# A graph layer on one core: rows copied before edges, scatters that wait for products, transposes moved behind a half's products

## The chip, the cores and the metric

The kernel runs on one core of one Trainium2 chip. A core has a matrix engine (TensorE, PE in the rows), a vector engine (VectorE, DVE), a scalar engine (ScalarE, ACT), GpSimd (POOL) and a queue engine (SyncE, SP). Each works through its own list of instructions in order; they meet through counters that an instruction raises at its end and another waits for. The metric is the device time of one execution in microseconds (us), lower is better.

## The reference

For 100,000 edges between 6,250 nodes, each with 128 features, a message is made from the source row, the destination row and the edge's own features, and the messages of a node are added up:

```python
row, col = (edge_index[0], edge_index[1])
msg_in = jnp.concatenate([x[row], x[col], edge_attr], axis=-1)
h = msg_in @ W + b
mu = jnp.mean(h, axis=-1, keepdims=True)
var = jnp.mean(jnp.square(h - mu), axis=-1, keepdims=True)
h = (h - mu) * jax.lax.rsqrt(var + LN_EPS) * gamma + beta
msg = jax.nn.relu(h)
out = jax.ops.segment_sum(msg, row, num_segments=x.shape[0])
# and around it: x = _layernorm(x + out)
```

The edges come sorted by `dst` (`col`), not by `src` (`row`), by which they are summed.

## The kernel before, in words

**Tables.** W is cut in three: x times its first third (`tabA`) and x times its second third (`tabB`) are made once, for 6,250 nodes. What is left for each edge is its own 128 features times the last third, plus two table rows.

**Groups and halves.** The edges are taken in 98 groups of 1,024 (`g` from 0 to 97), each as two halves of 512 (`h` 0 and 1); `t = 2 * g + h` counts halves. For a half:

- TensorE transposes the edges (`turn_edges`, L856, counter `e_turned`), ScalarE copies them from PSUM to SBUF (`copy_edges`, L1145, counter `eT_ready`), TensorE multiplies them by the weights and adds the `tabB` rows of a window by a 0/1 matrix (`edges_times_w`, L962 and L969, counter `h_done`). I call the result the half's products.
- ScalarE copies the products into `stage` (`stage_rows`, L1149, counter `st_ready`), and a number for each row (`number_rows`, L1139).
- Places for the rows in a DRAM array `rows`, sorted by blocks of source nodes, are worked out: VectorE makes one-hot matrices, TensorE ranks them (`ranks_from_base`, L844 and L846), VectorE makes positions (L1534, L1540, L1546).
- When a whole group is staged, GpSimd writes it with eight indirect DMAs of 128 rows each (`scatter`, L683). I call these eight a burst.

**Pairs.** Eleven groups (22 halves) later, while further edges are multiplied, the sorted rows are read back in pairs of units, `s = t - 22`. For a pair, TensorE turns the selectors (`turn_selectors`, L930), ScalarE copies them (`copy_selT`, L1175), TensorE picks `tabA` rows with them (`select_tile`, L940), VectorE adds these to the rows (L1564), ScalarE sums squares (L1183) and takes roots (L1189), VectorE makes messages (L1580), and TensorE sums them by node (`sum_tile`, L916). VectorE adds the sums to a table (L1556). After the last group comes a drain of the remaining pairs and the last layer norm.

**What sets the order.** Nothing is scheduled by a tool: each engine's `step` is written out by hand for all 98 groups, and the text of `step` is the order. Rings of four buffers hold edges, windows and staged rows; the edge loads run three groups ahead (`AHEAD`). The lines that wait, and that the change touches, are these:

```python
pool.wait_ge(st_ready, 2 * g + (1 if early else 2))     # scatter, GpSimd
pe.wait_ge(eT_ready, 2 * g + h + 1)                     # edges_times_w, TensorE
pe.wait_ge(st_ready, 2 * g + h - 1)
act.wait_ge(e_turned, 2 * g + h + 1)                    # copy_edges, ScalarE
act.wait_ge(h_done, 2 * g + h + 1)                      # stage_rows, ScalarE
```

The `Else` branches are for inputs whose destinations do not fit the windows; the input here takes the first branch.

## Time and profile before

| | |
|---|---|
| device time, median of 3 runs | 1757.65 us (1756.3 to 1757.97) |
| the profiled execution | 1758.61 us, its span 1756.8 us |
| busy share of the span | PE 68%, weight loads 60%, DVE 54%, POOL 44%, ACT 40% |
| granted TensorE clock, mean | 0.812 of full speed |
| chain that ended last | PE 39%, unknown queue 24%, issue 18%, ACT 10% |

No engine is busy all the time, so the time lies in how they wait for each other. The rows further down are read from the profile of this one execution. "Idle before" is how long an engine stood still ahead of an instruction, and the name behind the arrow is what ended it; "issue" means that nothing in the profile did, "remote" that the counter was raised by something the profile cannot name.

### The profile page before, as it was taken

Reading aid. Unit: us, or ns where it says so; the run is one execution under the profiler, and the core shown is the slowest. Engines: PE = TensorE matmul, PEld = TensorE weight load, DVE = VectorE, ACT = ScalarE, POOL = GpSimd, SP = SyncE. Lnnn points to the kernel's source line nnn. Section 1 sums busy time; section 2 is a strip of 40 time slices with the busy share of each in tenths; the row PEclk is TensorE's granted clock in tenths of the full one; section 3 lists DMA queues with packets and bytes.
Section 4 is the critical chain, followed back from the end, with each engine's and each line's share of the span. In section 5 each row is a group of like instructions: output and inputs, shape, how many; then the busy total and the mean of one; then the engine's idle time right before and its main releaser. Section 6 shows DMA issues by size and latency. Waiting matters only on the chain.

```text
span 1756.8 us, 36181 instructions
## 1 busy us (share of the span) xinstructions
PE 1201.1 (68%) x9913; PEld 1049.7 (60%) x9914; DVE 949.3 (54%) x2787; ACT 711.4 (40%) x2814; POOL 771.9 (44%) x810
## 2 busy tenths in 40 slices
PE   6598776666766666766666666667666667656775
PEld 5455666655666556666566666566555656655662
DVE  7623355545555445554455555455455455538997
ACT  3223343433434333443334333344344344335766
POOL 0335544455444455444554444554445554450003
PEclk9767777878878788787888778788888777878998
DMA  7665455344443444444444443444444444312322
GB/s 213 170 129 137 127 154 147 111 127 131 129 115 116 124 131 129 120 115 125 126 130 130 115 128 113 131 130 127 112 120 126 131 128 128 111 54 80 92 65 73
DMA packets 192458, 215.22 MB, mean 123 GB/s; under 512 B 51350, under 2 KB 141802, under 8 KB 192272
## 3 DMA queue, kind: packets, MB, share of 16 engines
q1 hardware_dynamic: 166236, 160.39, 35.1%
q0 software_dynamic: 25088, 51.83, 8.5%
q8 instruction: 83, 1.36, 0.3%
q14 instruction: 103, 0.84, 0.2%
q10 hardware_dynamic: 948, 0.79, 0.2%
HBM read 144.85 MB, written 68.06 MB: 121 GB/s over the span
## 4 chain that ended last, share of the span: by engine, by line
PE 39%; another core or an unknown queue 24%; issue 18%; ACT 10%; DVE 6%; DMA 2%; DVEq 1%; SPq 0%; ACTq 0%
PE bank L962 11%; PE bank L940 7%; PE bank L916 7%; ACT late L1183 5%; PE bank L856 5%; PE bank L930 3%; PE bank L969 2%; ACT turn L1145 1%; DVE late L1580 1%; PE bank L846 1%; DMA tabB<-room 1%; PE bank L844 1%; ACT late L1189 1%; DVEq L493 1%
## 5 line engine op out<-in xcount | busy, mean ns | idle before, releaser
L683 POOL DMA_INDIRECT rows<-p,pos_idx x784 | 756.0, 964 | 825.3 <-ACT p L1149 535.0
L1145 ACT COPY turn<-bank 128x512 f32<-128x512 f32 x196 | 115.0, 587 | 688.0 <-remote 523.3
L962 PE MATMUL bank<-wc,turn 128*128 128x128 f32 x1552 | 297.2, 351 | 66.9 <-ACT turn L1145 59.9
L940 PE MATMUL bank<-room 128*128 x2592 | 246.4, 250 | 106.6 <-issue 61.4
L962 PEld LDWEIGHTS bank<-wc,turn 128*128 128x128 f32 x1552 | 257.4, 251 | 88.1 <-ACT turn L1145 79.3
L940 PEld LDWEIGHTS bank<-room 128*128 128x128 bf16 x2592 | 204.3, 115 | 128.0 <-issue 117.6
L1183 ACT ACTIVATE late<-room 128x128 f32<-128x128 f32 x864 | 256.4, 303 | 2.7 <-issue 1.3
L916 PE MATMUL bank<-late 128*128 128x129 f32 x1472 | 230.3, 299 | 33.9 <-issue 31.4
L1580 DVE SCALAR_TENSOR_TENSOR late<-room,late,floor 128x128 f32<-128x128 f32 x864 | 248.1, 349 | 0.4 <-issue 0.3
L916 PEld LDWEIGHTS bank<-late 128*128 128x128 f32 x1472 | 207.5, 214 | 26.4 <-issue 26.0
L1175 ACT COPY room<-bank 128x512 bf16<-128x512 bf16 x216 | 127.0, 588 | 223.9 <-remote 128.8
L1564 DVE TENSOR_TENSOR room<-bank,room 128x512 f32<-128x512 f32 x128 | 88.0, 688 | 185.8 <-remote 185.1
L856 PE MATMUL bank<-ident,p 128*128 128x128 f32 x784 | 147.9, 321 | 35.8 <-issue 35.4
L1183 ACT ACTIVATION_READ_ACCUMULATOR late<-room 128x1 f32 x864 | 166.3, 192 | 0.0
L1564 DVE TENSOR_TENSOR room<-bank,late 128x512 f32<-128x512 f32 x88 | 60.5, 687 | 193.2 <-remote 193.1
L846 PE MATMUL bank<-turn,before 128*128 128x50 bf16 x704 | 55.4, 201 | 126.4 <-issue 126.4
L856 PEld LDWEIGHTS bank<-ident,p 128*128 128x128 f32 x784 | 102.1, 167 | 62.3 <-issue 61.3
L846 PEld LDWEIGHTS bank<-turn,before 128*128 128x128 bf16 x704 | 40.6, 110 | 163.7 <-issue 163.7
L1556 DVE TENSOR_TENSOR room<-room,bank 128x129 f32 x432 | 124.1, 287 | 26.2 <-issue 21.8
L1149 ACT COPY p<-bank 128x512 f32<-128x512 f32 x196 | 112.1, 572 | 4.4 <-PE bank L969 3.2
L930 PE MATMUL bank<-ident_bf,late 128*128 128x128 bf16 x736 | 82.9, 241 | 41.0 <-DVE late L1589 25.8
L969 PE MATMUL bank<-win,turn 126*128 126x128 bf16 x784 | 97.2, 260 | 0.8 <-issue 0.8
(240 smaller groups left out, 1256.1 us busy)
## 6 DMA issues: line engine op xcount, KB each, us to landing
p<-in_edge_attr_dram SPq DMA_DIRECT2D x98, 512.0 KB
room<-rows SPq DMA_DIRECT2D x256, 129.0 KB
near_bc<-near SPq DMA_DIRECT2D x98, 256.0 KB
late<-rows SPq DMA_DIRECT2D x176, 129.0 KB
rows<-p,pos_idx POOLq DMA_INDIRECT x784
win<-tabB SPq DMA_DIRECT2D x196, 31.5 KB
rows<-fill SPq DMA_DIRECT2D x24, 193.5 KB
tabB<-room SPq DMA_DIRECT2D x12, 384.0 KB, 3.8
```

Of the source, the lines that this page charges most:

```text
L683: nc.gpsimd.indirect_dma_start(rows_ap, bass.IndirectOffsetOnAxis(pos_idx[:, k, j:j + 1], 0), stage[:, k, j, :], None).then_inc(st_free[k] ...
L856: mm = pe.transpose(bank[E_BANK][:, t * P:(t + 1) * P], e_sb[:, k, j * D:(j + 1) * D], ident[:])
L916: mm = pe.matmul(o[:, jj // UJ, :], sel[kk][:, jj, :], msg_room[:, o_at(s, c, -2), jj, :], start=(jj % UJ == 0), stop=(jj % UJ == UJ - 1))
L930: mm = pe.transpose(turned[:, j * P:(j + 1) * P], sel_top[sel_at(s, c, 1, fused)][:, j, :], ident_bf[:])
L940: mm = pe.matmul(bank[A_BANK + b2][:, jj * D:(jj + 1) * D], selT[b2][:, jj * P:(jj + 1) * P], tabA[:, bass.ds(at[jj // UJ], 1), part, :], ...
L962: pe.matmul(bank[H_BANK + h][:, t * D:(t + 1) * D], eT[h][:, t * P:(t + 1) * P], wc[:, 2, :], start=(t == 0), stop=False, skip_group_check ...
L969: mm = pe.matmul(bank[H_BANK + h][:, t * D:(t + 1) * D], pick_t, win[0:WR, k, h, :], start=False, stop=(t == 3), skip_group_check=True)
L1145: nc.scalar.copy(eT[h], bank[E_BANK][:]).then_inc(eT_ready, 1)
L1175: nc.scalar.copy(selT[b2], turned).then_inc(n_selTc, 1)
L1183: a = nc.scalar.activation(junk[b2][:, j, :], pre[b2][:, j, :], ACT.Square, accum_out=ssq[:, b2, j:j + 1])
L1564: nc.vector.tensor_tensor(pre[b2], bank[A_BANK + b2][:].rearrange("p (j d) -> p j d", j=SJ), hs[kk][:, :, 0:D], ALU.add).then_inc(n_pre, 1)
L1580: a = nc.vector.scalar_tensor_tensor(msg_room[:, b2, j, 0:D], pre[b2][:, j, :], rstd[:, b2, j:j + 1], floor[:], ALU.mult, ALU.max)
```

## The change

Four edits, in three engines' lists:

- ScalarE's `step` copies finished rows (`stage_rows`) ahead of the next edges (`copy_edges`) in each half, and numbers the rows at the end of the first half instead of in the second.
- GpSimd's `scatter` waits for the rows of the first half (`st_ready`) and for the products of the second (`h_done`), issues four scatters, then waits for the rows of the second half and issues four more. `settle` steps a counter behind each of the two waits.
- TensorE's `step` transposes the edges of half `t + 1` directly behind the products of half `t`, and no more at the start of half `t + 1`.
- For group 0, which has no group ahead of it, the order is written as before.

```diff
@@ scatter, GpSimd
-            def scatter(g, k):
+            def scatter(g, k, windowed=False):
                 pool.wait_ge(pos_ready, g + 1)
                 pool.wait_ge(lo_ready, g + 1)
-                early = isinstance(g, int) and g == 0
-                pool.wait_ge(st_ready, 2 * g + (1 if early else 2))
+                pool.wait_ge(st_ready, 2 * g + 1)
+                if windowed and not (isinstance(g, int) and g == 0):
+                    pool.wait_ge(h_done, 2 * g + 2)
                 settle()
                 for j in range(COLS):
-                    if early and j == COLS // 2:
-                        pool.wait_ge(st_ready, 2)
+                    if j == COLS // 2:
+                        pool.wait_ge(st_ready, 2 * g + 2)
+                        settle()
                     nc.gpsimd.indirect_dma_start(rows_ap, ...)
...
-                every_group(lambda g, k, u: scatter(g, k))
+                every_group(lambda g, k, u: scatter(g, k, True))
@@ step, TensorE
-                        if g > 0:
-                            turn_edges(g, k, u, h)
-                        elif h == 0:
+                        t = 2 * g + h
+                        if t == 0:
                             first_edges(0)
                             first_edges(1)
-                        t = 2 * g + h
...
                         edges_times_w(g, k, h)
+                        if 0 < t < 2 * NG - 1:
+                            turn_edges((t + 1) // 2, slot(k, h), u + (k + h) // RING, (t + 1) % 2)
                         if selecting:
                             select_a(s, c, at)
@@ step, ScalarE
+                        if h == 1 and g > 0:
+                            stage_rows(g, k, 0)
+                        elif h == 0 and g > 0:
+                            stage_rows(g - 1, slot(k, -1), 1)
                         copy_edges(g, h)
+                        if h == 1 and not g > 0:
+                            stage_rows(g, k, 0)
...
-                        if h == 1:
-                            number_rows(g, k, u)
                         if not below(s, 1, 0):
                             copy_selT(s, c)
                         if not below(s, 0, 0):
                             squares(s, c)
-                        if h == 0 and not below(g, 0, 1):
-                            stage_rows(g - 1, slot(k, -1), 1)
-                        if h == 1:
-                            stage_rows(g, k, 0)
                         if not below(s, 0, 0):
                             roots(s, c)
+                        if h == 0:
+                            number_rows(g, k, u)
```

**TensorE, in the middle of the kernel.** The rows run from the last products of one group to the first products of the next. `bank3` and `bank2` hold the products of a second and a first half, `bank1` the transposed edges, `p1` the edges as loaded, `late` and `turn` selectors, messages and transposed operands. Before, where a line of "..." stands for further rows of the same operation and for the selections L940:

```order
L962 MATMUL bank3<-wc,turn 128x128 [waits rows_staged,eT_copied]
...
L969 MATMUL bank3<-win,turn 128x128 x4
...
L856 MATMUL bank1<-ident,p1 128x128 [waits eT_copied,e_loaded1]
...
L916 MATMUL bank7<-late 128x129 [waits runs_made,messages_made]
...
L844 MATMUL bank4<-cum,ident 128x50 [waits ranks_read,block_onehot_made,selectors_made]
L846 MATMUL bank4<-turn,before 128x50 x8
L930 MATMUL bank4<-ident_bf,late 128x128 [waits selT_copied,selectors_made]
...
L962 MATMUL bank2<-wc,turn 128x128 [waits rows_staged,eT_copied]
...
L969 MATMUL bank2<-win,turn 128x128 [waits window_loaded1,dst_selectors_made]
```

In the changed kernel (the same lines lie two further down: L856 is L858, L962 is L964):

```order
L964 MATMUL bank3<-wc,turn 128x128 [waits rows_staged,eT_copied]
...
L971 MATMUL bank3<-win,turn 128x128 x4
L858 MATMUL bank1<-ident,p1 128x128 [waits eT_copied,e_loaded1]
...
L918 MATMUL bank7<-late 128x129 [waits runs_made,messages_made]
...
L846 MATMUL bank4<-cum,ident 128x50 [waits ranks_read,block_onehot_made,selectors_made]
L848 MATMUL bank4<-turn,before 128x50 x8
L932 MATMUL bank4<-ident_bf,late 128x128 [waits selT_copied,selectors_made]
...
L964 MATMUL bank2<-wc,turn 128x128 [waits rows_staged,eT_copied]
...
L971 MATMUL bank2<-win,turn 128x128 [waits window_loaded1,dst_selectors_made]
```

The four transposes L858 now stand ahead of the selections, the sums L918 and the ranks, and the selector transposes L932 follow those as before.

**ScalarE, from the start of a first half to the squares of the second.** `bank2` and `bank3` are the products, `turn` receives the transposed edges, `room` the selectors. Before:

```order
L1145 COPY turn<-bank1 128x512 [waits edges_multiplied,e_turned]
L1175 COPY room<-bank4 128x512 [waits a_rows_selected,selectors_turned]
L1183 ACTIVATE late<-room 128x128 [waits rstd_made,pre_made]
L1183 ACTIVATE late<-room 128x128 x3
L1149 COPY p1<-bank3 128x4x128 [waits edges_multiplied]
L1189 ACTIVATE late<-late,eps128 128x4 [waits squares_summed]
L1145 COPY turn<-bank1 128x512 [waits edges_multiplied,e_turned]
L1139 COPY p1<-lo_f 128x8 [waits rows_scattered2]
L1175 COPY room<-bank4 128x512 [waits a_rows_selected,selectors_turned]
L1183 ACTIVATE late<-room 128x128 [waits rstd_made,pre_made]
L1183 ACTIVATE late<-room 128x128 x3
L1149 COPY p1<-bank2 128x4x128 [waits edges_multiplied]
```

In the changed kernel (L1145 is L1147, L1149 is L1151):

```order
L1151 COPY p1<-bank3 128x4x128 [waits edges_multiplied]
L1147 COPY turn<-bank1 128x512 [waits edges_multiplied,e_turned]
L1177 COPY room<-bank4 128x512 [waits a_rows_selected,selectors_turned]
L1185 ACTIVATE late<-room 128x128 [waits rstd_made,pre_made]
L1185 ACTIVATE late<-room 128x128 x3
L1191 ACTIVATE late<-late,eps128 128x4 [waits squares_summed]
L1141 COPY p1<-lo_f 128x8 [waits rows_scattered2]
L1151 COPY p1<-bank2 128x4x128 [waits edges_multiplied]
L1147 COPY turn<-bank1 128x512 [waits edges_multiplied,e_turned]
L1177 COPY room<-bank4 128x512 [waits a_rows_selected,selectors_turned]
L1185 ACTIVATE late<-room 128x128 [waits rstd_made,pre_made]
L1185 ACTIVATE late<-room 128x128 x3
```

The row copy L1151 has moved from behind the squares to the place ahead of the edge copy L1147, and the row numbers L1141 stand at the end of a first half.

## Rows read from the trace of the kernel before

**Rows 1.** Source view of L683 (scatters), then L1145: durations ns, count; idle ended by.

```profile
L683 POOL DMA_INDIRECT rows<-p,pos_idx x729: 956/962/1090, 132.8 to 1549.2; - x183
...
  ACT p L1149: 504.6, 90
...
  remote: 498.7, 86
```

**Rows 2.** Timeline of POOL: start us, length us, line, operation, [idle before, releaser].

```profile
811.33 0.96 POOL L683 DMA_INDIRECT rows<-p,pos_idx  x1 [0.30 <-issue]
818.16 0.96 POOL L683 DMA_INDIRECT rows<-p,pos_idx  x1 [5.87 <-ACT p L1149]
819.43 0.96 POOL L683 DMA_INDIRECT rows<-p,pos_idx  x1 [0.30 <-issue]
...
827.11 0.96 POOL L683 DMA_INDIRECT rows<-p,pos_idx  x1 [0.30 <-issue]
```

**Rows 3.** Timeline of ACT, same stretch and columns.

```profile
814.25 0.59 ACT L1145 COPY turn<-bank 128x512 f32<-128x512 f32 x1 [5.03 <-remote]
...
815.50 0.31 ACT L1183 ACTIVATE late<-room 128x128 f32<-128x128 f32 x1
...
816.68 0.57 ACT L1149 COPY p<-bank 128x512 f32<-128x512 f32 x1
817.15 0.30 ACT L1189 ACTIVATE late<-late,eps 128x4 f32<-128x4 f32 x1
819.56 0.59 ACT L1145 COPY turn<-bank 128x512 f32<-128x512 f32 x1 [2.11 <-PE bank L856]
820.05 0.21 ACT L1139 COPY p<-lo_f 128x8 f32<-128x8 f32 x1
821.05 0.59 ACT L1175 COPY room<-bank 128x512 bf16<-128x512 bf16 x1 [0.80 <-PE bank L930]
...
829.88 0.59 ACT L1145 COPY turn<-bank 128x512 f32<-128x512 f32 x1 [6.40 <-remote]
```

**Rows 4.** Timeline of PE, same stretch and columns.

```profile
814.02 0.53 PE L846 MATMUL bank<-turn,before 128*128 128x50 bf16 x8
...
814.89 2.08 PE L962 MATMUL bank<-wc,turn 128*128 128x128 f32 x8
816.76 0.63 PE L969 MATMUL bank<-win,turn 126*128 126x128 bf16 x4
817.19 1.49 PE L940 MATMUL bank<-room 128*128 x12
818.47 1.06 PE L856 MATMUL bank<-ident,p 128*128 128x128 f32 x4
819.32 1.47 PE L916 MATMUL bank<-late 128*128 128x129 f32 x8
820.63 0.39 PE L930 MATMUL bank<-ident_bf,late 128*128 128x128 bf16 x4
820.85 1.11 PE L962 MATMUL bank<-wc,turn 128*128 128x128 f32 x8
821.80 0.39 PE L969 MATMUL bank<-win,turn 126*128 126x128 bf16 x4
822.03 0.86 PE L940 MATMUL bank<-room 128*128 x12
823.41 0.63 PE L856 MATMUL bank<-ident,p 128*128 128x128 f32 x4 [0.53 <-issue]
```

**Rows 5.** Timeline of DVE, same stretch and columns.

```profile
829.83 0.69 DVE L1564 TENSOR_TENSOR room<-bank,late 128x512 f32<-128x512 f32 x1 [4.85 <-remote]
```

**Rows 6.** Windows: busy us of PE, PEld, DVE, ACT, POOL; clock, DMA share, GB/s.

```profile
814.00:820.00 6.00, 6.00 (x45) 5.77 (x45) 5.44 (x14) 3.45 (x13) 1.53 (x2) 0.50 0.32 79
```

**Rows 7.** Timeline of POOL, then ACT, near 1040 us.

```profile
1039.02 0.96 POOL L683 DMA_INDIRECT rows<-p,pos_idx  x1 [1.86 <-issue]
...
1043.31 0.59 ACT L1145 COPY turn<-bank 128x512 f32<-128x512 f32 x1 [3.16 <-remote]
```

## The prediction

> **What bounds the kernel now.** I read the page's slices first: outside the first and the last hundred microseconds every slice looks alike, so one group of 1,024 edges is the thing to understand. Its beat is set by GpSimd (POOL in the rows). [rows 1] count its scatters: 729 starts from 132.8 to 1549.2 us are 91 whole groups of eight, (1549.2 - 132.8) / 91 = 15.57 us a group. Eight scatters take only 9.9 us of that ([rows 2]: 818.16 to 827.11 + 0.96 = 828.07). For the rest POOL stands idle, and each time it is the copy of rows on L1149 that lets it go on (90 times, 504.6 us).
>
> Why is that copy late? In the timeline of ScalarE (ACT) [rows 3] the copy of transposed edges on L1145 starts at 814.25 after 5.03 us of idleness and at 829.88 after 6.40 us, both put down to "remote", a releaser that the profile cannot name; 86 waits of L1145 in these groups are such [rows 1]. What it waits for is L856, the transposes on TensorE. Those stand in TensorE's timeline [rows 4] at 823.41, over by 824.04, and yet ACT goes on at 829.88. The other event that fits is POOL's: the last scatter ends at 812.29, ACT resumes 1.96 us later; it ends at 828.07, ACT resumes 1.81 us later. VectorE shows the same: L1564 needs the row selection L940 that TensorE ended at 822.89 [rows 4], and starts at 829.83, after 4.85 us [rows 5]. So, whatever the mechanism, what TensorE finishes well inside a burst of scatters is seen by the other engines only when the burst is over. Not all of it: the transposes over at 819.53 release ACT at 819.56, 1.4 us after the burst's first scatter [rows 3, 4], and the selector transposes over at 821.02 release it at 821.05, 2.9 us after. L940, 4.7 us after, is withheld. I call the moment when ACT resumes the release. The limit lies between 2.9 and 4.7 us.
>
> A period is then two pieces. From release to first scatter: 814.25 to 818.16, 3.91 us. From first scatter to next release: 818.16 to 829.88, 11.72 us. Together 15.63, the mean being 15.57.
>
> **The change part by part.**
> (1) ScalarE copies the finished rows first, then the edges. In the first piece the rows of the second half are now copied at the release and not behind L1145, L1175 and four squares: that copy starts 816.68 - 814.25 = 2.4 us earlier. Taken alone, a gain of 2.4 us a group.
> (2) The first four scatters no longer wait for that copy but for the products of the second half, one half later than the rows that they write. The question is on which side of the burst those products fall. Before, they were made inside the burst (L962 and L969 of 820.85 to 822.19) and were seen at the release for nothing. To have them seen before a burst that itself starts 0.9 us after a release, both halves' chains, transpose, copy, product, would have to pass in one free stretch. One such chain passes in it (below), and the second one's transposes end too late: at least 1.16 us of copies, then products and transposes at the slow clock, 2.50 + 0.85, makes 4.6 us after a release, 3.7 us after the first scatter, past 2.9; and behind them the second half needs one more exchange, its selector transposes L930, before ACT, which works in order, comes to its rows. So I expect the kernel to settle where the release shows the first half's products and the second half's transposes, and ACT must do two copies (0.57 + 0.59 us), TensorE the second half's products, and only then POOL starts. TensorE's clock decides the products: after the idle end of a burst the granted clock is 0.50 [rows 6], which of the two levels is 1.2 GHz, and L962 with L969 take 814.89 to 817.39 = 2.50 us; at the full clock, 2.4 GHz, 820.85 to 822.19 = 1.34 us. From the end of the event that POOL waits for to its first scatter take 816.68 + 0.57 = 817.25 to 818.16, 0.91 us. Release to first scatter is then 0.57 + 0.59 + 0.05 (from 814.25 + 0.59 to 814.89) + 2.50 + 0.91 = 4.62 us, against 3.91: **0.71 us more** per group; at the full clock 3.46 us, 0.45 less. I take the slow clock, since the stretch behind the release shows it and TensorE still idles in the burst.
> (3) A second wait with a counter step stands in the middle of eight scatters. Scatters follow each other at 0.30 us [rows 2]; behind a wait it is 0.91. The cost is between 0 (all hidden behind the scatter before it) and 0.61 us; I take **0.3**. The rows it waits for are copied 0.57 us after the first four were allowed, long before the fifth's turn at about 5 us.
> (4) The next half's transposes stand directly behind a half's products, ahead of L940, L916 and the ranks. The instructions are the same. What this hides is the copy L1145: at the start of a burst it is done by ACT while TensorE selects and sums, so products of the first half are finished inside the burst. If that cover were gone, the cost would be one more copy, 0.59 us. SP's next edge load may be issued earlier; the loads are three groups ahead and no row of L1145 or L962 is released by one, so nothing.
> Sum of the likeliest case: 0.71 + 0.3 = 1.01 us x 91 = 92 us. The profiled execution took 1758.6 us (span 1756.8), the median is 1757.65; 1758.6 + 92 = **1851 us**. Front and drain, outside the 91 groups, are unchanged.
>
> **A step that can fail.** For that case ScalarE must get its selector transposes (L930 to L1175) inside the burst; they are now TensorE's last work before the limit. Behind the products come L856, L940, L916, the ranks and L930. Slow clock, in [rows 4]: L856 0.85 and L916 1.31 (start to the next start), L940 1.28, ranks 0.53, L930 0.39, less the 0.20 by which products overlap what follows = 4.2 us, 3.3 us behind the first scatter: between 2.9 and 4.7. Full clock, in the ratio of 1.34 to 2.50: 2.2 us, 1.3 behind it: passes. If they are withheld, ACT, which works in order, has L1175, squares, roots and the row numbers still to do after the release: 0.59 + 1.18 + 0.30 + 0.21 = 2.3 us in front of everything.
>
> One rule speaks against my reading. L1145 waits for the nameless releaser in 86 of 91 groups [rows 1], and in the two looked at it resumes 1.8 to 2.0 us behind the last scatter [rows 2, 3]; so I hold the two tied. The Trainium skill (SBUF — State Buffer, the section on its two separate sides) says that engine ports and DMA ports are disjoint and that a DMA cannot be slowed by a compute op, nor the reverse. By the rows the sum is the 1851 us above. By that rule the scatters' transfers hold nothing up, the withheld stretch has another cause, and the time could be that of the open burst, the third rival below; the trace shows no such cause, so that rival stays small.
>
> **The rivals.**
> - *Selector transposes withheld.* 2.3 us more in the groups it hits. A longer release-to-scatter piece gives TensorE time to come back to the full clock, so I expect every other group: 1.01 + 1.15 = 2.2 us x 91 = 197, **1955 us**; in every group 3.3 x 91 = 301, 2060 us. For it: 3.3 us is past what passed. Against: 4.7 is the first withheld.
> - *The full clock (other side).* One mechanism: TensorE, with less waiting ahead of the release, enters it at 1.0. Then 3.46 + 0 to 0.61 against 3.91: -0.45 to +0.16 us, 1718 to 1773 us, with the 0.3 of part 3 -0.15 x 91, **1745 us**. It decides where the products take under 1.49 us (3.91 - 0.57 - 0.59 - 0.05 - 0.91 - 0.3). Against: [rows 6].
> - *The burst lets more through.* With a pause after four scatters, or with the loads falling elsewhere, the second half's transposes are seen inside the burst. Then both products are ready at the release, and a period is 11.72 + 0.91 + 0.3 = 12.9 us: -2.6 x 91 = -240, **1518 us**. For it: at 1039.02 a scatter came 1.86 us late, and in that burst ACT's L1145 resumed at 1043.31 [rows 7], inside it. Against: the pause is five times shorter here (0.3 against 1.86 - 0.30), and that one let a single copy through.
> - *Nothing changes*: the gain of part 1 and the wait of part 2 cancel, 1758.
>
> **How the numbers follow.** Likeliest case 0.37, transposes withheld 0.22, full clock 0.2, burst lets through 0.15, cancel 0.06. Range: from the full clock's low end to the withheld case with the middle wait at 0.6 (2.5 us x 91 = 228): 1715 to 1985, which leaves out the 0.15 of the open burst and a little above. Within 0.2% (3.5 us), about what a measurement of this kernel can tell from no change: half of cancel and a sixth of full clock, 0.06. Faster: open burst 0.15, two thirds of full clock 0.13, a fifth of cancel, 0.3. Slower: the rest, 0.64.
>
> **What would show it.** In the new profile: POOL's first scatter of a burst released by L969's successor (products) and no more by the row copy; release to first scatter near 4.6 us; the gap between fourth and fifth scatter 0.3 to 0.9 us; at the release ACT does row copy, then edge copy, then TensorE the products at clock 0.5; L1175's counterpart starts inside the burst (likeliest) or first at the release (first rival). The prediction is wrong if periods come near 13 us, if the idle time labelled "remote" shrinks, or if the scatters are no longer followed by the release at 1.9 us.

## The result and the profile after

The changed kernel takes 1840.99 us (median of 4 runs, 1836.13 to 1850.33); the kernel before, on the same chip, 1756.97 us (4 runs, 1753.57 to 1757.97). The ratio is 1.0488 with a 95% interval of 1.0443 to 1.0533: the change makes the kernel 4.9% slower, 84 us. The prediction was 1851 us, with a range of 1715 to 1985.

The page of the profile after: the totals, the chain that ended last, and the groups of the lines that the change moves. Lines behind the scatters have moved by two to four: L1147 is the edge copy (before L1145), L1151 the row copy (L1149), L1177 the selector copy (L1175), L964 and L971 the products (L962, L969), L858 the edge transposes (L856). In kernels with further lines added they stand lower still (the selector copy is L1179 in the split kernel, L1183 in the pause kernel); the operation and the names in a row stay the same.

```profile
span 1841.0 us, 36279 instructions
...
another core or an unknown queue 38%; PE 27%; ACT 15%; issue 13%; DVE 4%; DMA 1%; DVEq 1%; ACTq 0%
...
L685 POOL DMA_INDIRECT rows<-p,pos_idx x784 | 760.0, 969 | 910.2 <-ACT p L1151 447.6
...
L1177 ACT COPY room<-bank 128x512 bf16<-128x512 bf16 x216 | 127.5, 590 | 668.4 <-remote 564.6
...
L1151 ACT COPY p<-bank 128x512 f32<-128x512 f32 x196 | 114.1, 582 | 272.8 <-remote 232.1
...
L1147 ACT COPY turn<-bank 128x512 f32<-128x512 f32 x196 | 115.6, 590 | 16.7 <-PE bank L858 16.0
```

Scatters still take 0.97 us each; what has grown is POOL's idle time, from 825.3 to 910.2 us, and the share of the chain that the profile can give no name to, from 24% to 38%. The edge copy, which before was released 86 times by "remote" [rows 1], has hardly a wait left: 16.7 us in all. The nameless waits have gone to the selector copy (564.6 us) and to the row copy (232.1 us).

The source view of the scatters, from the first steady group on (duration in ns, then the first and the last start):

```profile
L685 POOL DMA_INDIRECT rows<-p,pos_idx x745: 952/958/1212, 130.0 to 1663.7; - x187
```

745 starts are 93 whole groups and one start more: (1663.7 - 130.0) / 93 = 16.49 us a group, against 15.57 [rows 1]. 0.92 us in each of 91 groups is 84 us, the whole difference. (Counted from the very first to the very last burst the kernel after is 89 us longer, and the drain behind it 5 us shorter.) So one group explains it. The timelines of POOL, ACT and PE around one burst (start us, length us, then what the engine did, and in brackets how long it stood idle and what ended that):

```profile
846.92 0.96 POOL L685 DMA_INDIRECT rows<-p,pos_idx  x1 [6.31 <-ACT p L1151]
...
850.93 0.96 POOL L685 DMA_INDIRECT rows<-p,pos_idx  x1 [0.30 <-issue]
852.19 0.95 POOL L685 DMA_INDIRECT rows<-p,pos_idx  x1 [0.31 <-issue]
...
855.98 1.00 POOL L685 DMA_INDIRECT rows<-p,pos_idx  x1 [0.31 <-issue]
```

```profile
842.35 0.58 ACT L1151 COPY p<-bank 128x512 f32<-128x512 f32 x1 [5.16 <-remote]
842.83 0.59 ACT L1147 COPY turn<-bank 128x512 f32<-128x512 f32 x1
...
846.01 0.59 ACT L1151 COPY p<-bank 128x512 f32<-128x512 f32 x1 [0.61 <-PE bank L971]
...
852.73 0.59 ACT L1177 COPY room<-bank 128x512 bf16<-128x512 bf16 x1 [5.38 <-remote]
...
858.60 0.58 ACT L1151 COPY p<-bank 128x512 f32<-128x512 f32 x1 [3.70 <-remote]
```

```profile
843.47 2.08 PE L964 MATMUL bank<-wc,turn 128*128 128x128 f32 x8 [0.96 <-ACT turn L1147]
845.34 0.63 PE L971 MATMUL bank<-win,turn 126*128 126x128 bf16 x4
...
848.57 0.38 PE L932 MATMUL bank<-ident_bf,late 128*128 128x128 bf16 x4
848.79 1.11 PE L964 MATMUL bank<-wc,turn 128*128 128x128 f32 x8
```

From the release, 842.35, to the first scatter, 846.92, pass 4.57 us, in five steps: the row copy until ACT starts the next (0.48), the edge copy (0.59), the step to TensorE (0.05), the products (843.47 to 845.97, 2.50 us), and from their end to the scatter 0.95. The profile names the row copy L1151 as the releaser of the burst. It is not: it ends at 846.60, 0.32 us before the scatter, and in [rows 2, 3] a row copy that does release POOL ends 0.91 us before. The products end 0.95 us before. The profile puts a wait for several things down to one of them, and the times of the ends tell which it was. From the first scatter at 846.92 to the next release at 858.60 it is 11.68 us, as before. And the selector transposes L932 are over at 848.95, 2.0 us behind the first scatter, while the copy that waits for them starts at 852.73: late, but inside the burst, whose last scatter ends at 856.98. In 52 of the 56 groups between 600 and 1500 us the copy starts inside the burst: 1.9 to 5.9 us behind the first scatter in 28 of them (median 4.4), about 7.2 in 7, and 8.6 to 10.1 in 17 (median 9.3). In the other four it starts only at the release, 11.6 us behind the first scatter. In these four the burst ahead had stopped for 1.9 to 2.2 us behind its first scatter, its period is only 14.0 to 14.4 us, and the next one is 18.3 to 19.4 us: the two together are as long as two others.

|---|---|---|
| selector transposes L930 | 821.02 | 821.03 |
| products L969 | 822.19 | 829.68 |
| selections L940 | 822.88 | 829.80 |
| edge transposes L856 | 824.04 | 829.86 |
| sums L916 | 827.12 | 829.96 |

The four late ones go up within 0.3 us of each other, in the order in which TensorE did the work. In the kernel after it is the same: the products and transposes that end at 850.12 and 850.57 are counted at 858.58 and 858.64, and ACT resumes at 858.60. Taken over the 80 groups from the 13th to the 92nd of the kernel before, 423 of TensorE's 812 recorded counter steps come more than 0.1 us behind the end of the work, the latest 9.0 us; of ScalarE's 542 and VectorE's 921 (about a third of theirs have no record) none comes more than 0.02 us behind.

### The profile page after: what moved, and what is told of

It reads as the page before. It is cut to its first block, busy times and chain, and to the rows that moved or that the text cites. A ratio compares the mean times of both kernels' runs of the same rounds, so it can differ in the third digit from the quotient of the medians.

```text
span 1841.0 us, 36279 instructions
## 1 busy us (share of the span) xinstructions
PE 1209.8 (66%) x9913; PEld 1060.2 (58%) x9914; DVE 946.4 (51%) x2787; ACT 726.2 (39%) x2814; POOL 775.9 (42%) x810
## 4 chain that ended last, share of the span: by engine, by line
another core or an unknown queue 38%; PE 27%; ACT 15%; issue 13%; DVE 4%; DMA 1%; DVEq 1%; ACTq 0%
PE bank L964 8%; ACT late L1185 7%; PE bank L918 5%; PE bank L942 4%; ACT turn L1147 3%; PE bank L858 3%; PE bank L971 2%; PE bank L932 1%; ACT p L1151 1%; DVE late L1584 1%; ACT late L1191 1%; ACT room L1177 1%; DMA tabB<-room 1%; DVEq L493 1%
## 5 line engine op out<-in xcount | busy, mean ns | idle before, releaser
L685 POOL DMA_INDIRECT rows<-p,pos_idx x784 | 760.0, 969 | 910.2 <-ACT p L1151 447.6
L942 PE MATMUL bank<-room 128*128 x2592 | 251.6, 254 | 344.6 <-issue 202.5
L1177 ACT COPY room<-bank 128x512 bf16<-128x512 bf16 x216 | 127.5, 590 | 668.4 <-remote 564.6
L964 PE MATMUL bank<-wc,turn 128*128 128x128 f32 x1552 | 287.6, 343 | 65.8 <-ACT turn L1147 63.8
L1538 DVE TENSOR_TENSOR prod<-turn,bank 128x400 f32<-128x400 bf16 x98 | 55.9, 571 | 503.2 <-issue 299.9
L918 PE MATMUL bank<-late 128*128 128x129 f32 x1472 | 275.0, 335 | 59.2 <-issue 55.4
L964 PEld LDWEIGHTS bank<-wc,turn 128*128 128x128 f32 x1552 | 252.0, 246 | 85.6 <-ACT turn L1147 83.3
L918 PEld LDWEIGHTS bank<-late 128*128 128x128 f32 x1472 | 236.2, 239 | 71.1 <-issue 69.9
L1151 ACT COPY p<-bank 128x512 f32<-128x512 f32 x196 | 114.1, 582 | 272.8 <-remote 232.1
L858 PE MATMUL bank<-ident,p 128*128 128x128 f32 x784 | 145.2, 315 | 6.4 <-issue 6.2
L932 PE MATMUL bank<-ident_bf,late 128*128 128x128 bf16 x736 | 89.0, 248 | 68.6 <-issue 43.5
L1147 ACT COPY turn<-bank 128x512 f32<-128x512 f32 x196 | 115.6, 590 | 16.7 <-PE bank L858 16.0
L1568 DVE TENSOR_TENSOR room<-bank,late 128x512 f32<-128x512 f32 x88 | 60.6, 689 | 102.9 <-remote 80.0
L932 PEld LDWEIGHTS bank<-ident_bf,late 128*128 128x128 bf16 x736 | 59.7, 113 | 87.6 <-issue 53.6
L858 PEld LDWEIGHTS bank<-ident,p 128*128 128x128 f32 x784 | 102.9, 167 | 7.9 <-issue 7.9
L971 PE MATMUL bank<-win,turn 126*128 126x128 bf16 x784 | 92.7, 249 | 5.8 <-issue 5.8
```

The lines of the kernel that those rows point to most:

```text
L685: nc.gpsimd.indirect_dma_start(rows_ap, bass.IndirectOffsetOnAxis(pos_idx[:, k, j:j + 1], 0), stage[:, k, j, :], None).then_inc(st_free[k] ...
L858: mm = pe.transpose(bank[E_BANK][:, t * P:(t + 1) * P], e_sb[:, k, j * D:(j + 1) * D], ident[:])
L918: mm = pe.matmul(o[:, jj // UJ, :], sel[kk][:, jj, :], msg_room[:, o_at(s, c, -2), jj, :], start=(jj % UJ == 0), stop=(jj % UJ == UJ - 1))
L932: mm = pe.transpose(turned[:, j * P:(j + 1) * P], sel_top[sel_at(s, c, 1, fused)][:, j, :], ident_bf[:])
L942: mm = pe.matmul(bank[A_BANK + b2][:, jj * D:(jj + 1) * D], selT[b2][:, jj * P:(jj + 1) * P], tabA[:, bass.ds(at[jj // UJ], 1), part, :], ...
L964: pe.matmul(bank[H_BANK + h][:, t * D:(t + 1) * D], eT[h][:, t * P:(t + 1) * P], wc[:, 2, :], start=(t == 0), stop=False, skip_group_check ...
```

## The experiments

The experiments ran in five sets; each is compared with runs of the kernel before in its own set, since the sets are not alike: the kernel before took 1756, 1244, 1740, 1739 and 1738 us. The second one is told apart below.

**First set: one part of the change at a time, and a split burst.** The first three kernels are the kernel before with one part of the change: `pe` only moves the edge transposes, `act` only changes ScalarE's order, `pool` only the waits of the scatters. What was expected of them:

> The kernel before with TensorE's part of the change alone: the next half's edge transposes stand directly behind a half's products. My theory, the held-back signals: what TensorE raises from some 2 to 3 us after a burst's first scatter reaches the other engines only about 1.9 us after its last one, so a group lasts 11.7 us up to this release plus ScalarE's and TensorE's work from there to the next first scatter. The transposes stood at 0.4 us behind the first scatter and were seen; moved behind the products they are not on the way from the release to the next burst: 1745 to 1775 us, no change of more than 1%. Rival, the order on TensorE is what costs: most of the 84 us appear here, 1820 to 1850.

> The kernel before with ScalarE's part alone: the row copies stand ahead of the next edge copy, the row numbers in the other half; the first scatter still waits for both halves' rows, and TensorE's transposes stay. Held-back signals: at the release ScalarE copies rows first, then edges, then TensorE multiplies the second half at half clock (2.5 us), and then the second row copy has to follow before the first scatter: release to first scatter 4.6 us plus 0.6 for the row copy behind the products, against 3.9 before: some 1.2 us in each of 91 groups, 1840 to 1890 us. Rival, the cost sits in the waits ahead of the scatters: 1745 to 1765, or the 2.4 us less that I gave this part alone.

> The kernel before with the scatters' part alone: the first four wait for the first half's rows and the second half's products, the other four for the second half's rows. Held-back signals: ScalarE's order at the release is that of before (edge copy, products, row copy), so the first scatter comes no earlier than the products and at most the 0.57 us of the row copy ahead; but the row copy for the middle wait then stands among signals that are held back or not, so 0 to +1 us a group: 1700 to 1850 us. Rival, the waits cost by themselves (the middle wait and its increment, 0.3 us a group, and the wait for the products): the whole 84 us or more here, while the act kernel stays at 1757.

| kernel | us, median | ratio to before, 95% interval |
|---|---|---|
| before | 1756.35 | |
| pe | 1765.45 | 1.0051 (1.0033 to 1.0070) |
| act | 1865.12 | 1.0639 (1.0588 to 1.0690) |
| pool | 1738.02 | 0.9906 (0.9875 to 0.9936) |

ScalarE's order alone brings a loss larger than that of the whole change; the other two parts stay within 1%. The release stands in the timeline of ACT and then of POOL in the `act` kernel:

```profile
1361.26 0.59 ACT L1149 COPY p<-bank 128x512 f32<-128x512 f32 x1 [7.24 <-remote]
1361.74 0.59 ACT L1145 COPY turn<-bank 128x512 f32<-128x512 f32 x1
...
1364.93 0.59 ACT L1149 COPY p<-bank 128x512 f32<-128x512 f32 x1 [0.61 <-PE bank L969]
```

```profile
1366.43 0.96 POOL L683 DMA_INDIRECT rows<-p,pos_idx  x1 [6.79 <-ACT p L1149]
```

5.17 us from release to first scatter: the same steps as in the changed kernel, and one more row copy, since here the burst waits for both halves' rows. This one does end 0.91 us before the scatter.

The small gain of the `pool` kernel goes with something that the changed kernel does not have: with ScalarE's old order its middle wait is a real one. In 60 of its 98 bursts the gap ahead of the fifth scatter is over 0.5 us, in many of them 4 to 5 us, while in the changed kernel it is so in 3. So this part alone already breaks up many of the bursts, as the next kernel does on purpose; that the gain comes from it was not tested apart.

The fourth kernel is the changed kernel with one wait more:

```diff
                     if j == COLS // 2:
                         pool.wait_ge(st_ready, 2 * g + 2)
+                        if windowed and g < NG - 1:
+                            pool.wait_ge(h_done, 2 * g + 3)
                         settle()
```

> The changed kernel, and the fifth scatter of a group also waits for the products of the next group's first half. Those products end 3.3 us behind the first scatter. Held-back signals, tied to the scatters that are under way: they are seen about 1.9 us after the fourth scatter, at 5.7 us, the last four run from 5.8 to 9.6, and the work of one half (row copy, edge copy, products) is done between, so that what is left after the second release at 11.5 us is less than the 4.6 us of the changed kernel: a group of 12 to 15.5 us, 1480 to 1750 us in all. If the hold is not tied to the scatters but to time or to TensorE's idling, the middle wait adds what the fifth scatter waits: the release comes 11.7 us behind the first scatter in any case, and the last four only then: 20 us and more a group, over 2100 us.

It took 1594.14 us (1590.29 to 1596.49), a ratio of 0.9073 (0.9035 to 0.9111) to before. A wait added to the slow kernel made it 247 us faster. A steady group in its timelines of POOL, ACT and PE:

```profile
1308.58 0.95 POOL L687 DMA_INDIRECT rows<-p,pos_idx  x1 [1.96 <-remote]
...
1312.36 0.96 POOL L687 DMA_INDIRECT rows<-p,pos_idx  x1 [0.31 <-issue]
1315.41 0.96 POOL L687 DMA_INDIRECT rows<-p,pos_idx  x1 [2.09 <-issue]
...
1319.34 0.96 POOL L687 DMA_INDIRECT rows<-p,pos_idx  x1 [0.30 <-issue]
1322.25 0.96 POOL L687 DMA_INDIRECT rows<-p,pos_idx  x1 [1.96 <-remote]
```

```profile
1314.52 0.59 ACT L1179 COPY room<-bank 128x512 bf16<-128x512 bf16 x1 [3.92 <-remote]
...
1321.22 0.59 ACT L1179 COPY room<-bank 128x512 bf16<-128x512 bf16 x1 [3.56 <-remote]
```

```profile
1311.37 1.11 PE L966 MATMUL bank<-wc,turn 128*128 128x128 f32 x8
1312.31 0.39 PE L973 MATMUL bank<-win,turn 126*128 126x128 bf16 x4
...
1317.92 1.11 PE L966 MATMUL bank<-wc,turn 128*128 128x128 f32 x8
1318.87 0.39 PE L973 MATMUL bank<-win,turn 126*128 126x128 bf16 x4
```

There are two releases, at 1314.52, 1.20 us behind the end of the fourth scatter, and at 1321.22, 0.92 us behind the eighth. In each stretch of four one half's products are made, at the full clock (1.34 us, 1317.92 to 1319.26), and are there when the release comes; the next burst starts 1.03 us behind it and not 4.57. This group lasts 1322.25 - 1308.58 = 13.67 us; the mean is 13.8, since the middle wait varies: in 12 of 80 groups in the middle of the kernel the gap is 3.7 to 5.0 us. The expectation had the middle release at 5.7 us behind the first scatter (it is 5.94) and a group of 12 to 15.5.

**Second set: no held-back signals.** Three more kernels combine the parts and the split, and one has a pause in place of the wait:

> The changed kernel with ScalarE's part undone (its order is that of before: edge copy, ..., row copy), TensorE's and the scatters' parts made. Alone, ScalarE's part cost 109 us, the scatters' part gave 18 and TensorE's cost 9. If the parts add up: 1757 + 9 - 18 = about 1748 us (1730 to 1770), and the loss of the changed kernel is ScalarE's order. If instead the moved transposes and the new waits meet in a new chain (the transposes now stand behind products that are themselves held back), 1800 to 1900 us.

> The changed kernel with TensorE's part undone: the edge transposes stand ahead of the products again. By adding up 1757 + 109 - 18 = 1848 us, about the time of the changed kernel. By the chain at the release: the transposes of a half are then ahead of its products at the start of a burst or behind the release, and the edge copy behind the row copy has to wait for them: 1840 to 1980 us. Under 1800 would say that TensorE's order is what makes the changed kernel slow, beside ScalarE's.

> The kernel before, in which the fifth scatter also waits for the products of the next group's second half, which TensorE ends 3.4 us behind the first scatter; nothing else. Held-back signals: the wait ends about 1.9 us after the fourth scatter, and the second stretch of four starts at 5.8 us instead of 5.1; what was late until 11.7 us (selector transposes, edge copy) gets done in the middle. The split of the changed kernel brought 1841 down to 1594 us; here some 1550 to 1700 us. If the gain there needed the changed order, the split costs its 1.7 us a group here: 1880 to 1920 us.

> The changed kernel with 14 small GpSimd memsets (8 columns each, chained) between the fourth and the fifth scatter, some 2 to 4 us, and no wait for another engine there. If it is the scatters under way that hold TensorE's signals back, a pause without any wait for them lets them through as well: the group is then like that of the split kernel, 1560 to 1700 us, though GpSimd does more. If the split kernel gained because of what it waited for, or if GpSimd's being busy with anything holds the signals back, the pause is added to each group: 1841 + 98 times 2 to 4 us, over 2000 us.

None of these expectations could be tested. The kernel before itself ran at 1244.42 us (21 runs, 1239.39 to 1249.81), on a chip that the results list under the same number as that of the first set. `pe_pool` took 1248.96 us (1.0045, 1.0025 to 1.0064), `act_pool` 1242.52 (0.9976, 0.9957 to 0.9996), `before_split` 1245.29 (1.0008, 0.9984 to 1.0032), `pause` 1448.21 (1.1642, 1.1617 to 1.1666). The page of `before_split` in this set, the chain and two groups:

```profile
DMA 21%; DVE 16%; issue 16%; POOL 15%; PE 12%; ACT 12%; DVEq 4%; SPq 3%; POOLq 0%; ACTq 0%
...
L685 POOL DMA_INDIRECT rows<-p,pos_idx x784 | 761.4, 971 | 325.7 <-issue 270.4
...
L1177 ACT COPY room<-bank 128x512 bf16<-128x512 bf16 x216 | 126.8, 587 | 94.0 <-PE bank L932 89.3
```

The nameless share of the chain is gone, and so are the nameless waits of the selector copy. In the counters' own record of the four kernels of this set none of TensorE's steps, between 860 and 878 in each over the same 80 groups, comes more than 0.02 us behind the end of its work. Scatters take the same 0.97 us, but POOL goes from one group to the next without a gap, and then nothing that ScalarE or TensorE do in another order matters. Eight scatters at 1.27 us from start to start are 10.1 us, and the mean group in the middle is 10.2 us. So the 4.9% of the change belong to sets in which signals are held back; the changed kernel as a whole was not run in one where they are not, but its parts were, two at a time.

**Third set: the pause again.** The changed kernel with this between the fourth and the fifth scatter, and no wait for another engine:

```diff
                         pool.wait_ge(st_ready, 2 * g + 2)
+                        if windowed:
+                            for i in range(14):
+                                pool.wait_ge(s_idle, 14 * g + i)
+                                nc.gpsimd.memset(idle[:], 0.0).then_inc(s_idle, 1)
                         settle()
```

> The changed kernel with the GpSimd pause between the fourth and the fifth scatter once more (2.55 us in the trace of its first run). The set in which it ran first had the kernel before at 1244 us, and in its traces no engine waited for held-back signals, so it could not tell anything. If the kernel before runs at about 1757 us this time: 1560 to 1660 us if the scatters under way hold TensorE's signals back (they come through in the pause, a group is 2 times 4.8 us of scatters, the pause and up to 2 us behind the eighth), 2030 to 2100 us if only waits for work bring the gain or if GpSimd's being busy holds them back. If the kernel before runs at 1244 us again: 1448 us again, GpSimd's 12.3 us a group.

The kernel before was at 1740.29 us in this set, the pause kernel at 1572.63 (1570.06 to 1575.19), a ratio of 0.9046 (0.8982 to 0.9110). The pause kernel has two runs here. POOL, then ACT:

```profile
789.94 0.95 POOL L691 DMA_INDIRECT rows<-p,pos_idx  x1 [0.30 <-issue]
790.89 2.23 POOL L690 MEMSET idle<- 128x8 f32 x14
793.27 0.96 POOL L691 DMA_INDIRECT rows<-p,pos_idx  x1
```

```profile
792.06 0.59 ACT L1183 COPY room<-bank 128x512 bf16<-128x512 bf16 x1 [3.89 <-remote]
```

ACT is released at 792.06, 1.17 us behind the fourth scatter and in the middle of the memsets: GpSimd is busy, no one waits, and the signals come through. So it is the stop of the scatters that lets them through; neither a wait nor an idle GpSimd is needed. 2.2 us of useless work in each group make the changed kernel some 268 us faster than it was (1841 us in the first measurement, 1573 us here, in another set). In the second set the kernel with the same pause is 16% slower than the kernel before.

**Fourth set: TensorE's and the scatters' parts together, and a wait that never waited.**

> ScalarE's part of the change undone, the other two made, in a set where the kernel before may run at 1757 us again. If it does: by adding up the parts 1757 + 9 - 18 = about 1748 us (1730 to 1775) if ScalarE's order alone is what loses the 84 us; if the moved transposes and the waits at the scatters meet in a new chain, 1800 to 1900 us. If the kernel before runs at 1244 us, 1249 us again.

> The kernel before with one wait more, the fifth scatter for the products of the next group's second half, in a set where the kernel before may run at 1757 us again. If it does: 1550 to 1700 us if the scatters under way hold the signals back (a release in the middle and one at the end, as in the split kernel's 1594 and the pause kernel's 1573 us), 1880 to 1920 us if the gain there needed the changed order and the wait only costs here. If the kernel before runs at 1244 us, 1245 us again: the wait costs nothing there.

Before 1739.30 us. `pe_pool` took 1679.73 (1667.19 to 1684.98), a ratio of 0.9657 (0.9604 to 0.9710): by their ratios alone (1.0051 times 0.9906) the two parts should give 0.4%, and they give 3.4%. Both cases of the expectation, 1730 to 1775 and 1800 to 1900 us, are missed. What they left out is the middle wait: in 56 of the 98 bursts the gap ahead of the fifth scatter is over 0.5 us, up to 5 us, so here too more than half of the bursts are broken up. With ScalarE's part on top, measured in another set, the ratio is 1.0488, so that part costs about 8.6% here (1.0488 / 0.9657) and 6.4% alone: it closes the middle wait again. How much each of these is worth was not measured apart. A row of its timeline shows that the hold is not watertight:

```profile
682.96 0.59 ACT L1147 COPY turn<-bank 128x512 f32<-128x512 f32 x1 [4.84 <-remote]
```

The burst runs from 674.35 to 684.55 without a gap, and the edge copy is released inside it, 8.6 us behind the first scatter. By the counters' record the products that end at 676.24 are counted at 681.53 and the transposes that end at 676.69 at 682.94: late, in their order, but ahead of the burst's end. The next in line, ended at 677.47, is counted at 685.85, behind it. What sets how many come through inside a burst isn't settled.

`before_split` took 1734.43 us, 0.9970 (0.9957 to 0.9982), and missed its expectation for a plain reason: the kernel was not what its text says. Its middle wait was for `2 * g + 3`, the products of the next group's first half, which in the order of before stand ahead of the burst. The gap ahead of its fifth scatter is 0.30 us in 97 of 98 groups. The run says only that a satisfied wait is nearly free.

**Fifth set: the middle wait on the right products.**

```diff
+                    if windowed and j == COLS // 2 and g < NG - 1:
+                        pool.wait_ge(h_done, 2 * g + 4)
```

> The kernel before with the middle wait on the right products. The kernel before_split waited at its fifth scatter for the next group's first half's products, which stand ahead of the burst there (they end at 14.7 us behind the first scatter of the burst before), so it never waited: in its trace the gap ahead of the fifth scatter is 0.30 us. Here the fifth scatter waits for the second half's, which end 3.5 us behind the first scatter. If the kernel before runs at about 1740 to 1757 us in this set: held-back signals give a wait until some 5.7 us behind the first scatter (a gap of 1 to 2.1 us in the middle), a release there, and a group of 12.5 to 14.5 us: 1500 to 1660 us. If a release in the middle is of use only in the changed order, or the products are seen at once, the gap stays near 0.3 and the time at 1730 to 1760 us; a wait without a release costs 1 to 2 us a group, 1830 to 1950 us. If the kernel before runs at 1244 us, 1240 to 1250 us.

1709.80 us (1708.21 to 1721.45) against 1738.36: 0.9856 (0.9818 to 0.9894), between the cases that I had put down: the release in the middle comes as expected, but the group stays at 15.1 us and not at 12.5 to 14.5. A group with a real middle wait, POOL and ACT:

```profile
750.24 0.96 POOL L685 DMA_INDIRECT rows<-p,pos_idx  x1 [5.30 <-ACT p L1151]
...
756.34 1.02 POOL L685 DMA_INDIRECT rows<-p,pos_idx  x1 [1.34 <-remote]
...
765.28 0.96 POOL L685 DMA_INDIRECT rows<-p,pos_idx  x1 [4.13 <-ACT p L1151]
```

```profile
762.15 0.59 ACT L1177 COPY room<-bank 128x512 bf16<-128x512 bf16 x1 [5.29 <-remote]
763.82 0.56 ACT L1151 COPY p<-bank 128x512 f32<-128x512 f32 x1
```

The split works (the wait ends at 756.34, 6.1 us behind the first scatter), but only about every second burst has it (55 of 98 with a gap over 0.5 us), and behind the second release the burst waits 3.13 us more: in ScalarE's old order the row copy stands behind the selector copy and four squares. It starts at 763.82 and not at 762.15. That is the 1.7 us which the change's new order would take away, and the split kernel, which has that order, starts its burst 1.03 us behind the release. So ScalarE's part costs in a whole burst, as the `act` kernel shows, and by these rows it should pay in a split one. The kernel that would show this by itself, the split kernel with ScalarE's old order, was not run.

## Why the prediction was right

Step by step, as it stands above:

- **The reading of the bound** (engines see what TensorE finishes well inside a burst only when the burst is over) holds. The split and the pause kernels show it: with four scatters at a time the release comes after each four. That it is tied to the scatters was argued before; now it is shown, in the sets where it occurs. The counters' record shows the lateness itself. The prediction's limit "between 2.9 and 4.7 us" was read from one burst; in the kernel before half of the steps that TensorE raises between 1 and 2 us behind the first scatter are already more than 0.1 us late, and of those raised between 3 and 5 us half are more than 7 us late. It is a slope and not a limit.
- **Release to first scatter**, 0.57 + 0.59 + 0.05 + 2.50 + 0.91 = 4.62 us, with the slow clock. Measured: 0.48 + 0.59 + 0.05 + 2.50 + 0.95 = 4.57, and 4.57 is also the median of 65 groups, from the 22nd on. Windows of the changed kernel (busy us of PE, PEld, DVE, ACT, POOL; then clock, DMA share, GB/s) show a mean clock of 0.66 around the products and of 1.00 behind the first scatter:

```profile
842.00:847.00 5.00, 3.75 (x25) 3.55 (x26) 3.67 (x11) 3.85 (x14) 0.08 (x1) 0.66 0.30 105
847.00:851.00 4.00, 3.57 (x46) 3.31 (x43) 1.09 (x2) 0.35 (x1) 3.09 (x4) 1.00 0.41 93
```

  The 0.66 is a mean of both levels: taken by single microseconds, the clock is 0.50 from 844 to 846 us, where the products run. L964 takes 2.08 us there, as at 0.50 before [rows 4, 6], and 1.11 us a little later at 1.00, where it is off the path. The rival "full clock" fell here.
- **The increase of 0.71 us** was too small: it is 0.93. The 3.91 us of before were read from one group; the median of the same 65 groups of the kernel before is 3.64. A row of ACT and one of POOL from its trace show the usual case:

```profile
674.64 0.59 ACT L1145 COPY turn<-bank 128x512 f32<-128x512 f32 x1 [8.21 <-remote]
```

```profile
678.27 0.96 POOL L683 DMA_INDIRECT rows<-p,pos_idx  x1 [5.20 <-ACT p L1149]
```

  678.27 - 674.64 = 3.63. A term that is a difference of two stretches needs the usual one of each.
- **The middle wait, 0.3 us**, costs nothing: in 95 of 98 bursts the fourth and the fifth scatter stand 0.30 us apart like all others (850.93 + 0.96 to 852.19). The two errors nearly cancel: 0.71 + 0.3 = 1.01 predicted, 0.93 + 0 against a mean of 0.92. That 1851 came so near to 1841 is therefore partly luck: both terms were off, in opposite directions, by 0.2 and 0.3 us a group, which is 20 and 27 us in all.
- **The step that could fail**, the selector transposes, went as in the likeliest case: they pass inside the burst, in 52 of 56 groups. The prediction had them over 3.3 us behind the first scatter, at the slow clock throughout; here they are over at 2.0 (1.7 to 3.5 in the 52 groups), since the clock is back at 1.00 from 847 us on. And they pass late, at 4.4, 7.2 or 9.3 us, and not at once as "passes" meant; the copy for them then has the nameless wait that the edge copy had. Since ACT has nothing on the path between them and the release, this costs nothing. The rival "transposes withheld" (1955 us) fell as a rule; it is there in the four groups of 18.3 to 19.4 us.
- **The gain of 2.4 us that the row copy alone was to bring** is not there when it is alone: the `act` kernel loses 6.4%. The prediction had counted it as part of a sum whose other members take it back; the row copy that the burst needs is the second half's, and the new order puts that behind the edge copy and the products.
- **What would show it** named the products as the releaser of a burst. The profile says so only in 9 waits (60.6 us) and names the row copy in 68; the times of the ends say so in the burst shown.
- The rival "the burst lets more through" was priced at 1518 us and given 0.15 for this change. It did not come of the change as a rule, but it is real: four of the five bursts between 600 and 1500 us that stop for 1.9 to 2.2 us by themselves have it (the four periods of 14.0 to 14.4 us, each paid back by a long one), and a pause of 2.2 us in the middle of every burst gives 1573 us.

## What to carry to other kernels

Where several engines resume together, after waits that the profile can't name, look for the event that all of them follow, and count as the path only what must happen between that event and its next start; work is cheap on one side of it and dear on the other, and an order that is right for one is wrong for the other. Before tuning such a wait away, run the unchanged kernel in several sets, at different times and on different chips: of six sets, counting that of the result, five had it at 1738 to 1757 us and one at 1244, and a change that wins 10% in the one can lose 16% in the other. And if a burst of indirect scatters of GpSimd has such a shadow, try to break it with a wait that is true at the right moment sooner than with a pause, which costs 16% where there is no shadow. That such a wait costs nothing there is not shown: the split kernel was not run in such a set, only a wait that was already satisfied, and that one cost nothing (1.0008).

## What the runs showed of the hardware

- While GpSimd issues indirect scatters, counters that TensorE raises go up late, in five of six sets. With eight scatters (9.9 us) the others resume 1.8 to 2.0 us behind the end of the last [rows 2, 3]; with four (4.7 us), 0.9 to 1.2 us. In the kernel before, what TensorE raises in the first 1 us of a burst is counted at once (within 0.36 us), between 1 and 3 us partly late, and from 3 us on nearly always when the burst is over, up to 9.0 us late; the steps come in the order of TensorE's work. Between a release and the next burst the steps are on time again (0.01 us is the usual lag). ScalarE's and VectorE's recorded steps are never late (0.02 us at most). A busy GpSimd alone does not do it (the memsets).
- What the delay is made of is open. The trace shows when the work ends by its own reckoning and when the counter goes up, and nothing between. Transfers under way are not enough by themselves: in the kernel before the last packet of a burst's scatters ends 0.9 us behind the last scatter (median) and the engines resume 1.0 us later, while in `before_split` in the second set packets still move 2.5 us behind the last scatter and no step is more than 0.02 us late.
- The Trainium skill (SBUF — State Buffer, the section on its two separate sides) would have engine ports and DMA ports apart, and so no slower engines under DMAs. In the rows that holds for the work: in the middle of a burst, at 848.79, L964 takes 1.11 us at a clock of 1.00, no more than its matmuls took in any row seen. It is the counter steps that are late, of which that section doesn't speak.
- The same kernel, with the same scatters of 0.97 us, took 1756 us in one set and 1244 us in another on a chip listed under one number. What makes a set the one or the other is open; the kernel is the same in both.
